# A state-space layer and a mixture-of-experts layer on one core: rounding part of softplus moved to ScalarE, a reordered scan stage, slot numbers kept in PSUM

## What is computed

```python
def ssm(ctx, z, ...):                       # z = layernorm(x)
    xr = einsum('ed,bld->bel', in_proj_w, ctx)
    u = silu(conv_4_taps(xr) + conv_b)
    B, C, dt_lo = x_proj(u)                 # 16, 16 and 8 rows
    delta = softplus(dt_proj_w @ dt_lo + dt_proj_b)
    for t in range(256):                    # 256 channels x 16 states, 4 batches
        state = state * exp(delta[t] * A) + (delta[t] * u[t]) * B[t]
        y[t] = (state * C[t]).sum(states)
    return (y + D * u) * silu(z)

x = x + ssm(ctx, layernorm(x), ...)
xn = layernorm(x)
probs = softmax(xn @ Wg); gates, chosen = top_k(probs, 2)
# each expert has 320 slots; a token's place is its rank among the expert's tokens
for e in range(8):
    out_e = relu(rows_of(e) @ w1[e]) @ w2[e]
x = x + sum over a token's two experts of gate * out_e
```

## Time and profile before

| | us |
|---|---|
| median of 3 runs | 314.25 (314.14 to 314.87) |
| profiled execution | 314.71 |
| its span | 312.6 |
| share of the span: PE, DVE, ACT, POOL | 85%, 70%, 54%, 70% |

### The profile page before, as it was taken

The page is one execution under the profiler, slowest core; times in us unless marked ns, Lnnn a source line. Parts: engine busy times, 40 slices in busy tenths (PEclk is TensorE's granted clock), DMA queues, the critical chain, the costliest instruction groups (busy, mean ns, idle before and its releaser), DMA issues. The chain is left out here.

```text
span 312.6 us, 4937 instructions
## 1 busy us (share of the span) xinstructions
PE 264.2 (85%) x1520; PEld 232.9 (75%) x1520; DVE 218.2 (70%) x383; ACT 170.0 (54%) x367; POOL 218.7 (70%) x182
## 2 busy tenths in 40 slices
PE   8969877886957947697699899999999999999960
PEld 7748665755746636576488799999999999999950
DVE  2489999987699788998945346857575757566610
ACT  1678579463893457638404347646473737373410
POOL 1839699959939699698371686677777777777652
PEclk9995989596796976756559999999999999999995
DMA  6459540052001442110055144454555454644011
GB/s 171 172 142 338 167 170 0 3 191 113 0 17 54 163 155 122 51 53 0 34 199 181 64 103 163 176 210 167 209 167 208 166 207 165 208 166 167 33 40 38
DMA packets 14929, 40.24 MB, mean 129 GB/s; under 512 B 2906, under 2 KB 9756, under 8 KB 11968
## 3 DMA queue, kind: packets, MB, share of 16 engines
q1 hardware_dynamic: 11648, 33.02, 31.2%
q0 software_dynamic: 2816, 6.32, 5.8%
q10 hardware_dynamic: 448, 0.70, 0.9%
HBM read 32.58 MB, written 8.49 MB: 131 GB/s over the span
## 5 line engine op out<-in xcount | busy, mean ns | idle before, releaser
L342 POOL TENSOR_TENSOR dbu<-du,bsb 128x1024 f32<-128x1024 f32 x31 | 72.5, 2359 | 6.2 <-ACT bsb L515 3.6
L1131 DVE TENSOR_TENSOR_SCAN h<-ps,dbu 128x512 f32<-128x512 f32 x64 | 74.5, 1206 | 1.1 <-ACT ps L529 0.7
L529 ACT ACTIVATE ps<-delta,anegs 128x255 f32<-128x255 f32 x128 | 53.0, 462 | 7.5 <-DVE h L1131 7.3
L1296 DVE SCALAR_TENSOR_TENSOR htlo<-ps,hthi 128x320 fp32r<-128x320 f32 x64 | 30.5, 487 | 35.2 <-ACT hthi L655 35.2
L766 PE MATMUL ps<-cst,hc 128*128 128x128 f32 x256 | 48.4, 351 | 0.0
L749 PE MATMUL ps<-stack,sels 64*128 64x256 f32 x64 | 19.5, 393 | 33.1 <-DVE hc L1142 29.6
L426 POOL TENSOR_TENSOR w2lo<-w2raw,w2hi 128x512 fp32r<-128x512 f32 x30 | 38.4, 1303 | 9.8 <-ACT w2hi L646 9.6
L766 PEld LDWEIGHTS ps<-cst,hc 128*128 128x128 f32 x256 | 39.4, 182 | 4.6 <-issue 2.2
L749 PEld LDWEIGHTS ps<-stack,sels 64*128 64x128 f32 x64 | 12.3, 239 | 40.6 <-issue 40.5
L935 PE MATMUL ps<-hthi,w2hi 128*128 128x320 f32 x128 | 40.3, 315 | 0.0
L935 PE MATMUL ps<-xthi,w1hi 128*128 (+1 forms) x128 | 40.2, 314 | 0.0
(11 more groups left out here) (149 smaller groups left out, 482.1 us busy)
## 6 DMA issues: line engine op xcount, KB each, us to landing
w1raw<-in_w SPq DMA_DIRECT2D x8, 1024.0 KB
w2raw<-in_w SPq DMA_DIRECT2D x8, 1024.0 KB, 4.8
bsb<-b_rows SPq DMA_DIRECT2D x7, 1024.0 KB, 7.3
expert_rows<-fill SPq DMA_DIRECT2D x1, 2580.0 KB, 15.9
xe<-expert_rows SPq DMA_DIRECT2D x8, 258.0 KB, 5.3
out<-x SPq DMA_DIRECT2D x4, 256.0 KB, 4.9
xnat<-in_x SPq DMA_DIRECT2D x1, 768.0 KB, 7.4
xe<-expert_rows SPq DMA_DIRECT2D x8, 64.5 KB, 5.5
```

The source lines that it names most:

```text
L342: nc.gpsimd.tensor_tensor(dbu[j % DRING][:], du[:, :, None, cols(b)].to_broadcast([P, EC, 2, L]), bsb[b % 2][:, None, 2 * p:2 * p + 2, :]. ...
L529: ins = nc.scalar.activation(decays(g % SLOTS_DA)[:, c, i * L + 1:(i + 1) * L], delta[:, c, b * L + 1:(b + 1) * L], ACT.Exp, scale=anegs[: ...
L1131: nc.vector.tensor_tensor_scan(h[g % HRING][:, c].rearrange("p n t -> p (n t)"), decays(g % SLOTS_DA)[:, c, :], dbu[g % DRING][:, c].rearr ...
L1296: nc.vector.scalar_tensor_tensor(out=htlo[:, f, :], in0=ps[:, f % 4, 0:CAP], scalar=0.0, in1=hthi[:, f, :].bitcast(F32), op0=ALU.max, op1= ...
```

## The change

The edits, grouped:
- **Softplus.** For batches 1 to 3 ACT makes the rounding part with two copies (`round_off`), between the exponential and the logarithm; POOL's `softplus_d` is gone. For batch 0 the bias is no longer a matmul: ACT adds it in |v|, in two halves, and DVE in max(v + bias, 0).
- **Bias and skip.** `dt_bias` and the skip term D*u (`open_sums`) are transposes instead of matmuls; the skip term is multiplied out by ACT (`skip_rows`, two instructions per batch), the bias comes by a new DMA into `dtb`. POOL's `diagd` is gone.
- **Prologue.** 2 and 6 dummy matmuls on PE stand before and after the product of the dt weights, where `dt_bias` stood.
- **Scan stage.** Many pieces have another p: `project` of batches 2 and 3 moves from the batch's own first pairs to p = 7 of two batches ahead, the gate of the logits and `choose` move a pair later, `place` keeps its p and its intermediates lie in PSUM, gate weights are made at p + 1 with the last product on ACT (`weigh`), `z_rstd(2)` and the second half of softplus on POOL move a pair later, `z_turn(3)` moves from p = 5 to p = 1, POOL's scatters are sent two at a time and later, the high part of expert 0's w1 is made earlier.
- **Between the stages.** The transposes of xnat move from the last pair to p = 5; the four dummy matmuls ahead of `counts(3)` are gone; PE waits for `slots_done` behind L1026 in place of ahead of it; ACT has `weigh(3)` ahead of its copies of expert 0's rows.

`choose(0)` stands one scan and one product later. The diff, cut to its core:

```diff
-    def softplus_d(b):
-        pool.wait_ge(s["sp_exp"], b + 1)
-        nc.gpsimd.tensor_scalar(spd, spe, 1.0, -1.0, ALU.add, ALU.add).then_inc(s["sp_d"], 1)
...
+        if b >= 1 and p == 0:
+            add_x(b - 1)
+        if b >= 1 and p == (1 if b == B - 1 else 2):
+            row_rstd(b - 1)
         if b >= 0 and b + 1 < B:
-            if p == (2 if b else 3):
-                softplus_d(b + 1)
+            if p == 3:
                 softplus_w(b + 1)
-            if p == 3:
+            if p == 4:
                 softplus_delta(b + 1)
                 delta_u(b + 1)
-        if b == 0 and p == 4:
+        if b == 0 and p == 5:
             z_rstd(2, slice(BT, TILES))
-        if b >= 1:
-            if p == 0:
-                add_x(b - 1)
-            if p == (1 if b == B - 1 else 2):
-                row_rstd(b - 1)
-            if p == 7:
-                if b == 1:
-                    pool.wait_ge(s["xe_filled"], 16)
-                send(b - 1)
+        if b == 2 and p in (1, 5):
+            if p == 1:
+                pool.wait_ge(s["xe_filled"], 16)
+            send(0 if p == 1 else 1)
+        if b == 3 and p in (2, 3):
+            send(p)
         drive(j)
-    send(B - 2)
...
+    for j in tiles_range(B - 2):
+        send(j)
...
+            nc.scalar.activation(spe, by_chunk(bank), ACT.Abs).then_inc(s["sp_abs"], 1)
+        else:
+            for c in range(EC):
+                nc.scalar.activation(spe[:, c, :], ps[:, bank + c, 0:L], ACT.Abs,
+                                     bias=ch[:, c, DTB:DTB + 1]).then_inc(s["sp_abs"], 1)
+        act.wait_ge(s["sp_abs"], EC + b)
         nc.scalar.activation(spe, spe, ACT.Exp, scale=-1.0).then_inc(s["sp_exp"], 1)
+    def round_off(b):
+        nc.scalar.activation(spd, spe, ACT.Copy, bias=1.0).then_inc(s["sp_s"], 1)
+        act.wait_ge(s["sp_s"], b)
+        nc.scalar.activation(spd, spd, ACT.Copy, bias=-1.0).then_inc(s["sp_d"], 1)
     def logs(b):
         act.wait_ge(s["sp_exp"], b + 1)
+        if b:
+            round_off(b)
         nc.scalar.activation(spl, spe, ACT.Ln, bias=1.0).then_inc(s["sp_ln"], 1)
...
+    def weigh(b):
+        act.wait_ge(s["weights_sum"], b + 1)
+        act.wait_ge(s["const_done"], 1)
+        for j in tiles_range(b):
+            ins = nc.scalar.activation(xrow[:, j, :, DM], etop[:, j, 0:TOPK], ACT.Copy,
+                                       scale=rsum[:, j:j + 1])
+        ins.then_inc(s["gates_done"], 1)
...
+    def skip_rows(b):
+        act.wait_ge(s["u_done"], EC * (b + 1))
+        if b:
+            act.wait_ge(s["opened"], b)
+        for c in range(EC):
+            ins = nc.scalar.activation(skip[:, c, :], u[:, c, cols(b)], ACT.Copy,
+                                       scale=ch[:, c, DSK:DSK + 1])
+        ins.then_inc(s["skip_done"], 1)
+    skip_rows(0)
...
-            silu_pieces(2, WBANK, range(BT, 3 * BT), 2)
+            silu_pieces(2, WBANK, range(BT, 2 * BT + 1), 2)
         if b == 1 and p == 6:
-            silu_pieces(3, WBANK, range(3 * BT, TILES), 2)
+            silu_pieces(3, WBANK, range(2 * BT + 1, TILES), 2)
+        if nb < B and p == 5:
+            skip_rows(nb)
         if nb < B:
             if p == (1 if b else 2):
                 b_rows(nb)
                 hi_rows(nb)
+            if p == 2:
                 decay_exps(nb, WBANK)
                 logs(nb)
         if b >= 1:
-            if p == (2 if b == B - 1 else 4):
+            if p == (2 if b == B - 1 else 3):
                 x1_turned(b - 1)
             if p == (3 if b == B - 1 else 5):
                 row_scales(b - 1)
-                top_exp(b - 1)
                 for j in range((b - 1) * BT, b * BT):
                     normalise(j)
-        if b == B - 1 and p == 5:
-            for m in range(WP):
-                split_w1(0, m)
-        if p == (7 if b < B - 2 else 6):
+            if p == (4 if b == B - 1 else 6):
+                top_exp(b - 1)
+            if p == (5 if b == B - 1 else 7):
+                weigh(b - 1)
+        if b == B - 1 and p in (1, 4):
+            for m in range(WP // 2):
+                split_w1(0, m + (WP // 2 if p == 4 else 0))
+        if p == (7, 7, 6, 2)[b]:
             z_turned(b)
...
-            nc.tensor.matmul(by_chunk(bank)[:, c, :], dts[0:1, 2 * DI + c * P:2 * DI + (c + 1) * P],
-                             onesf[0:1, 0:1].to_broadcast([1, L]), start=(c == 0), stop=False,
-                             skip_group_check=True)
+            for t in range(BT):
+                nc.tensor.matmul(by_chunk(bank)[:, c, t * P:(t + 1) * P], dtb[:, c * P:(c + 1) * P], ident,
+                                 start=(c == 0 and t == 0), stop=False, is_transpose=True,
+                                 skip_group_check=True)
...
+        pe.wait_ge(s["skip_done"], b + 1)
         for t in range(BT):
             for c in range(EC):
-                nc.tensor.matmul(y[:, t, c * P:(c + 1) * P],
-                                 u[:, c, b * L + t * P:b * L + (t + 1) * P], diagd[:, c, :],
-                                 start=(t == 0 and c == 0), stop=False, skip_group_check=True)
+                ins = nc.tensor.matmul(y[:, t, c * P:(c + 1) * P], skip[:, c, t * P:(t + 1) * P], ident,
+                                       start=(t == 0 and c == 0), stop=False, is_transpose=True,
+                                       skip_group_check=True)
+        ins.then_inc(s["opened"], 1)
...
+    keep_clock(2, BBANK)
...
-    dt_bias(V0BANK)
+    keep_clock(6, BBANK)
     pe.wait_ge(s["wdt_done"], 1)
     for k in range(EC):
         pe.wait_ge(s["u_done"], k + 1)
-        ins = dt_part(0, k, V0BANK)
+        ins = first_dt(k)
...
-            if p == (2 if b == B - 1 else 4):
+            if p == (3 if b == B - 1 else 4):
                 logits(b - 1)
-            if p == (3 if b == B - 1 else 5):
+            if p == (4 if b == B - 1 else 6):
                 counts(b - 1)
         if g + 1 < STEPS:
...
+        if b == 0 and p == 1:
+            pe.wait_ge(s["u_done"], EC * 2)
+            pe.wait_ge(s["wg_done"], 1)
+            pe.wait_ge(s["b_done"], CASTS)
+            pe.wait_ge(s["dtb_in"], 16)
+            project(1, XBANK[1])
+            dt_bias(WBANK)
+            dt_part(1, 0, WBANK)
+            dt_part(1, 1, WBANK).then_inc(s["v_psum"], 1)
+        if b >= 1 and nb < B:
+            if p == 0:
                 pe.wait_ge(s["zt_done"], b)
-            if b >= 2:
-                pe.wait_ge(s["slots_done"], b - 1)
-            project(nb, XBANK[nb])
-            dt_bias(WBANK)
-            dt_part(nb, 0, WBANK)
-            dt_part(nb, 1, WBANK).then_inc(s["v_psum"], 1)
+                dt_bias(WBANK)
+                dt_part(nb, 0, WBANK)
+            if p == 1:
+                dt_part(nb, 1, WBANK).then_inc(s["v_psum"], 1)
         if b + 2 < B and p in (3, 4):
             pe.wait_ge(s["sp_t"], nb + 1)
             conv(b + 2, p - 3, WBANK)
-        if p == (6 if b + 2 < B else 5):
-            pe.wait_ge(s["zs_done"], (1, 2, 2, 3)[b])
+        if p == (6, 6, 5, 1)[b]:
+            pe.wait_ge(s["zs_done"], (1, 2, 3, 3)[b])
             if b + 2 < B:
                 pe.wait_ge(s["u_done"], EC * (b + 3))
             elif nb < B:
             else:
                 pe.wait_ge(s["zt_done"], b)
             z_turn(b)
-        if b >= 1 and p == (1 if b == B - 1 else 3):
+        if b == B - 1 and p == 5:
+            pe.wait_ge(s["slots_done"], B - 1)
+            turn(xnat[:, tiles_of(B - 1), :], True, False)
+        if b + 2 < B and p == 7:
+            if b:
+                pe.wait_ge(s["slots_done"], b)
+            project(b + 2, XBANK[b + 2])
+        if b >= 1 and p == (1 if b == B - 1 else 2):
...
-    keep_clock(4, DABANK)
     counts(B - 1)
     place_rows(1)
-    pe.wait_ge(s["slots_done"], B)
-    pe.wait_ge(s["zt_done"], B)
...
+    for c in range(EC):
+        dve.wait_ge(s["sp_abs"], c + 1)
+        nc.vector.tensor_scalar(spt[:, c, :], ps[:, V0BANK + c, 0:L], ch[:, c, DTB:DTB + 1], 0.0,
+                                ALU.add, ALU.max).then_inc(s["sp_relu"], 1)
     dve.wait_ge(s["sp_exp"], 1)
     nc.vector.tensor_scalar(spd, spe, 1.0, -1.0, ALU.add, ALU.add).then_inc(s["sp_d"], 1)
-    softplus_t(0, V0BANK)
+    dve.wait_ge(s["sp_relu"], EC)
+    nc.vector.tensor_tensor(spt, spt, spe, ALU.add).then_inc(s["sp_t"], 1)
...
+        place_of = ps[:, BBANK, PLACEAT:PLACEAT + BT * NE].rearrange("p (t e) -> p t e", e=NE)
+        picked = ps[:, BBANK, PICKAT:PICKAT + BT * TOPK * NE].rearrange("p (t k e) -> p t k e", k=TOPK, e=NE)
+        slot = ps[:, BBANK, SLOTAT:SLOTAT + BT * TOPK].rearrange("p (t k) -> p t k", k=TOPK)
+        link(nc.vector.scalar_tensor_tensor(out=place_of, in0=over[:], scalar=DROPPED, in1=at,
                                             op0=ALU.mult, op1=ALU.add))
-        link(nc.vector.tensor_tensor(ohc[:, tiles, :, :], oh[:, tiles, :, :],
+        link(nc.vector.tensor_tensor(picked, oh[:, tiles, :, :],
```

(23 more changed lines are left out.)

71 lines of the change are left out of this document (33 added, 38 removed).

## The result

The changed kernel takes 301.07 us, median of 4 executions (300.90 to 302.52), beside 314.19 (312.95 to 314.87) for the kernel before on the same chip: a ratio of 0.960, 95% interval 0.956 to 0.964. The profiled execution took 302.52 with a span of 300.5, so -12.1 by the spans. The forecast of 302.9 against 314.7 was -11.8. A later series of runs gave 302.88 against 312.88, 0.965 (0.961 to 0.970). By the medians the gain is thus 13.1 us in the first series and 10.0 in the later one. The two series of one kernel differ by half a per cent, so where an experiment moves less than that, it is read from distances within its trace.

What follows compares the result with a forecast made beforehand. DVE was taken to set the pace up to the last scan, then PE's unchanged expert stage. Terms -12.8 to expert 0, +2.0 clock, +0.4 expert 0, -1.4 prologue sum to -11.8: 302.9 us from 314.7, 8-in-10 range 299.5 to 307.5.

Steps and rivals of the forecast that it cites:

- Waits that go: DVE's waits up to the last product, for logits, B and C rows, c_cast(31), Wg's sum and dbu(8), vanish: -15.8 us.
- Waits that come: New DVE waits in the scan stage, among them scan(9) +1.2 and step 13 +1.0: +3.5 us (0.4 to 6).
- the 13.4: DVE's last product of the scan stage ends 13.4 us sooner, with scan(0) held at 19.68.
- Overlap: On DVE, each of nine places losing its wait also saves about 0.1 us beyond its idle time: -0.9 us.
- Short instructions: On DVE, placing intermediates in PSUM and the last gate-weight product on ACT: -0.2 us over three batches (-0.6 to +0.3).
- The step that takes part back: Before expert 0, scatters behind w1lo delay the row load: PE waits 3.6 us, then a clock fall costs +2.0.
- Prologue: Dummy matmuls lift the clock before batch 0's dt_part, scan(0) 1.4 us sooner; if not, +1.1; little better than even.
- Transposes and the clock: Rule against the forecast: transposes don't count as busy PE, so batch 1's skip and bias would bring fewer clock rises; unsized.
- The quick load: Rival before expert 0: clock stays up and the load lands at 156.2, giving 300.0 us; chance 0.12.
- The low clock: Rival: PE at half speed in prologue, scan-stage waits and tail, giving 308.7 us, 306 with half of it; chance 0.23.
- Late scatters that PE never sees: Rival before expert 0: PE never sees the load's wait, giving 297 to 301 us; chance 0.09.
- ACT as the releaser of most scans: Sign of the slower rival: ACT's queue delays decays, 0.5 us a pair, giving 316 to 319 us; chance 0.06.

Runs made afterwards that it cites:

- the clock held: Changed kernel with 8 dummy matmuls on PE between the last logits and the first row placing: 300.50 us, ratio 0.963 of the kernel before.
- the scatters first: Changed kernel with POOL's four scatters of batch 2 ahead of the four w1lo again: 301.27 us, ratio 0.964 of the kernel before.
- the fastest version: Changed kernel with three w1lo ahead of batch 2's scatters, one behind, 10 and 4 PE dummy matmuls, z's statistics at p = 3: 296.84 us, 0.948 of before.
- the split of w1lo: Changed kernel with three of POOL's four w1lo ahead of batch 2's four scatters and the last behind: 299.73 us, ratio 0.958 of the kernel before.

## Why the prediction was right, step by step

- **Waits that go: right.** `lo_rows` 0, `choose` 0 within the scan stage, the sum of Wg 0, and two of the moves were undone one by one and brought 5.5 and 3.1 us back. The -8.0 for `choose` was right in size, but its new place by itself carries only some 3 of it; the rest went with the transposes of x1 and a shorter convolution, which the prediction doesn't name. The last product kept 0.81 of its 1.9 us: its cast no longer waits for `z_turned(3)`, but it stands behind the transposes of xnat, which the change put there, and runs at half speed (0.80 us; 0.47 is its length at full clock).
- **Waits that come: mis-sized.** Forecast 3.5, measured 4.8 with the rest on the last product. Scan(9) was put at 1.2 and took 1.61; step 13 at 1.0 and took 0.68; `choose(2)` and `softplus_t(2)` did not wait at all. What the sum did not have is the 1.08 us in batch 0, from a clock that had fallen behind an idle time of PE (3.10 us), and the last product's 0.81. The waits explain 1.3 of the 1.85 us that are missing from the 13.4.
- **Overlap: miscounted.** A place with a wait costs 0.09 us beyond the wait, since a product otherwise starts 2.25 us behind the start of its scan, which lasts 2.34. The sum took nine such places as gone and counted none among those that come. It was eight and seven, which makes -0.1 and not -0.9.
- **Short instructions: mis-sized.** The placing and the gate weights hold DVE for 1.44 us in the kernel before (in batch 3 from 150.60 to 152.04) and for 0.98 + 0.30 in the changed one (from 138.27 and from 142.62): -0.5 for three batches and not -0.2. With the overlap this is the other 0.5.
- **The step that takes part back: right in kind, half in size.** POOL's w1lo and the late scatters set the load. PE waited 1.80 and not 3.6: with scan(0) set to 19.68 it was free at 155.4 instead of 153.1, for the most part since DVE was 1.85 later than forecast. The load was there at 157.2 instead of 156.7, by two errors against each other: it was issued at 154.2 instead of 152.75, and took 3.05 us instead of 3.6 to 4. The fall of the clock was put at 2.0. From the first row placing to expert 0 it is 162.89 - 155.16 = 7.73 us, and 159.33 - 153.61 = 5.72 with the clock held: 2.0. The 0.5 for `weigh(3)` ahead of ACT's first copy shows as the 0.57 us for which PE waits for it once the clock is held.
- **Prologue: right, by the better of two cases.** Product for delta 3.78 to 1.97 us, scan(0) 2.05 sooner where 1.4 was said. The dummies account for 1.3 of it. Without them the product ends 0.6 us sooner than in the kernel before (12.47 against 13.07), which is most of the rest; no run says why.
- **The title's two parts.** The copies of softplus: forecast 0 on ACT and 0.35 for `dbu(8)`; measured 0.3 at most, at another scan, so the size is right by luck. The placing in PSUM: forecast "the length of one tiny instruction", -0.2, and this step was wrong in its reason. Against the kernel before the sum holds, because the product stayed at 0.20 us. But the -13.4 stood on it: without it, with the scatters moved, GpSimd holds the product for 0.73 + 6.66 + 6.97 - 3 x 0.20 = 13.8 us more and the cast for 1.9, of which 12.0 reach the end. In this the forecast came out by luck. The forecast weighed every moved instruction by what it waits for, and none by the engine that reads the same memory beside it.
- **Transposes and the clock.** No run separates them, since in every version PE's additions of the state are transposes and the rest is mixed between them. The mean granted clock is 0.866 before and 0.868 after, so there is no sign of fewer rises; the mean doesn't count them.
- **The rivals.** The quick load: it was quick (3.05 us), but issued late, and the clock did fall. The low clock was half there in batch 0 and not in the prologue. Late scatters that PE never sees fell with its wait of 1.80 us. ACT as the releaser of most scans isn't to be seen (2 waits, 2.3 us in all).
- **The total: partly luck.** -11.8 was forecast and -12.1 came by the spans, because terms that were off cancel: +1.85 up to the last product, -0.65 in the prologue, -1.3 from there to expert 0, -0.2 behind it. The last is not explained.

## What to carry to other kernels

An instruction's place is priced by more than what it waits for: look at what GpSimd does at that moment, and at whether VectorE's operation there takes all its inputs from SBUF. Such an operation, however small, may stand still for a whole row of GpSimd instructions; in this kernel a product, an add and a cast did. With an input in PSUM the product and the cast took 0.20 and 0.16 us beside the same `dbu`. The stand-still is no idle time in a profile: it shows as an instruction far longer than others of its line, which ends with one of GpSimd's. A short idle time of PE ahead of a serial chain costs twice, once as the wait and once as the clock behind it; dummy matmuls that last just as long as the wait give the second part back. And an order that failed (the scatters first) may hold the gain after all, once the trace shows what took it.

## What the hardware showed that was not expected

- A VectorE product of 128x32 with both inputs in SBUF took 6.66 and 6.97 us beside rows of three and five GpSimd instructions, 0.19 without, ending 0.06 us after the last of them both times; a third time it took 0.73 and ended between two. A cast of 128x4 from SBUF to SBUF took 2.03 in place of 0.17. A 128x512 add took 4.26 in place of 0.69 and ended 0.56 us behind the last w1lo; in the fastest version, where the last w1lo ran 0.3 us into it, it took 0.89 and ended 0.57 behind.
- An idle time of PE of only 1.80 us was followed by work at 1.2 GHz that cost 2.0 us. With the split of w1lo the idle time was 0.57 us, and the granted clock fell at 154 us all the same (0.55 from 154 to 155; eight matmuls in 3.65 us); four dummies in that place kept it up (2.42). On the other hand, about 3 us of idle time ahead of the same convolution left it anywhere between 1.98 and 3.76 us from profile to profile.
